# Attention inside a two-layer cross-attention and expert kernel: the transposed-score heads and the P.V groups run four slots behind the plain-score heads of the next batch

## The reference

```python
q = layernorm(x) @ Wq.T ; k = ctx @ Wk.T ; v = ctx @ Wv.T + bv      # 16 heads of 16
scores = einsum('bhsd,bhtd->bhst', qh, kh) / 4                      # masked with -inf
out = einsum('bhst,bhtd->bhsd', softmax(scores), vh)
x = x + tanh(g) * (out @ Wo.T + bo)
```

## Time and profile before

| | us |
|---|---|
| median of three runs (2249.01 to 2251.82) | 2249.69 |
| the profiled execution, own time | 2242.63 |
| its span | 2240.9 |
| layer 0, from the first step's `max_t` to the last one's | 75.2 to 542.6 |
| layer 1, the same | 1057.7 to 1545.8 |
| TensorE busy | 1637.9 (73%) |
| VectorE busy | 1236.0 (55%) |
| ScalarE busy | 665.6 (30%) |
| mean granted TensorE clock | 0.874 of full speed |

### The profile page before, as it was taken

The page is one execution under the profiler, slowest core; times in us unless marked ns, Lnnn a source line. Parts: engine busy times, 40 slices in busy tenths (PEclk is TensorE's granted clock), DMA queues, the critical chain, the costliest instruction groups (busy, mean ns, idle before and its releaser), DMA issues. The chain is left out here.

```text
span 2240.9 us, 44334 instructions
## 1 busy us (share of the span) xinstructions
PE 1637.9 (73%) x14427; PEld 1343.8 (60%) x14428; DVE 1236.0 (55%) x3261; ACT 665.6 (30%) x1299; POOL 724.0 (32%) x620
## 2 busy tenths in 40 slices
PE   3787778887575477735877877787463888896897
PEld 3676667665464355533555555554342888886897
DVE  3565556554466133344656656654465566667664
ACT  2233333333464011111433333343232222221221
POOL 4121112210476455541111111110386533334332
PEclk9989998998898799976888988988676999998999
DMA  3323333321222366644323323320622233332322
GB/s 105 106 88 89 90 104 88 87 78 31 102 94 99 83 116 107 107 91 111 92 84 91 96 78 87 89 74 16 217 78 76 61 66 75 75 75 66 75 35 40
DMA packets 166676, 191.78 MB, mean 86 GB/s; under 512 B 15442, under 2 KB 146868, under 8 KB 166324
## 3 DMA queue, kind: packets, MB, share of 16 engines
q1 hardware_dynamic: 135092, 149.69, 22.9%
q0 software_dynamic: 28416, 40.03, 9.9%
q10 hardware_dynamic: 3072, 0.79, 0.2%
HBM read 113.73 MB, written 75.67 MB: 85 GB/s over the span
## 5 line engine op out<-in xcount | busy, mean ns | idle before, releaser
L629 ACT ACTIVATE a_probs<-a_scores_t 128x384 f32<-128x384 f32 (+1 forms) x512 | 269.7, 545 | 524.7 <-PE a_scores_t L764 262.4
L1714 ACT ACTIVATE e_hidden<-e_h,t_up_bias 128x256 f32<-128x256 f32 x348 | 145.9, 470 | 564.7 <-PE e_h L1748 552.5
L550 DVE TENSOR_REDUCE a_row_max<-a_scores 128x2 f32<-128x512 f32 x256 | 170.3, 679 | 170.5 <-PE a_scores L749 169.0
L407 POOL TENSOR_TENSOR a_rest<-a_qk,a_parts 128x1024 f32<-128x1024 f32 x32 | 68.0, 2125 | 461.6 <-ACT a_parts L582 461.6
L1639 POOL DMA_INDIRECT out_rows<-e_y,e_token x68 | 112.5, 1654 | 309.9 <-DVE e_y L1697 289.9
L1763 PE MATMUL e_y_bank<-e_down_hi,e_hidden_hi 128*128 128x256 f32 x544 | 165.1, 304 | 64.2 <-DVE e_hidden_lo L1670 63.2
L767 PE MATMUL a_scores_t<-a_q_stack,a_k_stack 101*128 101x256 bf16 x512 | 115.7, 315 | 69.0 <-DMA a_q_stack<-a_max_t 67.2
L547 DVE TENSOR_REDUCE a_row_max<-a_scores 128x1 f32<-128x128 f32 x256 | 71.5, 279 | 168.7 <-PE a_scores L746 167.4
L1763 PE MATMUL e_y_bank<-e_down_hi,e_hidden_lo 128*128 128x256 f32 x544 | 159.6, 293 | 0.0
L1763 PE MATMUL e_y_bank<-e_down_lo,e_hidden_hi 128*128 128x256 f32 x544 | 159.4, 293 | 0.0
L1748 PE MATMUL e_h<-e_xs_hi,e_up_hi 128*128 128x256 f32 x544 | 155.9, 287 | 3.1 <-DVE e_xs_lo L1660 1.9
(11 more groups left out here) (257 smaller groups left out, 4539.9 us busy)
## 6 DMA issues: line engine op xcount, KB each, us to landing
parts_dram<-a_parts SPq DMA_DIRECT2D x32, 768.0 KB, 4.1
e_xs_rows<-routed_rows_dram SPq DMA_DIRECT2D x76, 258.0 KB, 2.7
a_q_stack<-parts_dram SPq DMA_DIRECT2D x64, 192.0 KB
a_k_stack<-parts_dram SPq DMA_DIRECT2D x64, 192.0 KB
a_ctx_rows<-in_ctx SPq DMA_DIRECT2D x32, 256.0 KB, 9.1
a_q_stack<-parts_dram SPq DMA_DIRECT2D x64, 128.0 KB
a_k_stack<-parts_dram SPq DMA_DIRECT2D x64, 128.0 KB
t_up<-in_L_ffn_W SPq DMA_DIRECT2D x8, 1024.0 KB, 5.2
```

The source lines that it names most:

```text
L550: nc.vector.reduce_max(row_max[:, :, h], bank[:].rearrange("p (c t) -> p c t", c=TC), AX_X).then_inc(maxed, 1)
L629: nc.scalar.activation(probs[h % NP][:, 0:width], scores_t[h % 2][:, 0:width], ACT.Exp).then_inc(probs_ready, 1)
L1714: nc.scalar.activation(hidden[:, fc, :], h_bank[g][:, at:at + TS], act_func, bias=routed.up_bias[:, bass.ds(e * FC + fc, 1)]).then_inc(hid ...
```

## The change

The transposed heads and everything that hangs on them move four slots back on TensorE; there are now 20 slots, where slots 0 to 3 hold plain heads alone and slots 16 to 19 transposed heads alone. The P.V groups 0, 1 and 2 come in slots 9, 13 and 17. The other parts keep their slot number, so that they stand four transposed heads earlier. ScalarE's parts, which count exponentials, get other numbers to fit, and `cut_hi` comes ahead of all exponentials. VectorE inverts and divides group pair 0 of batch i behind the split of the maxima. POOL waits for its own last result before it writes `rest` again.

```diff
+    LAG = 4
@@ POOL
                     pool.wait_ge(part_hi, b + 1)
+                    need(pool, parts_ready, b)
@@ VectorE
-                if i.has(0):
-                    between |= {14: lambda: invert_dens(0, 0, 0), 15: lambda: (invert_dens(0, 0, 1), divide(0, 0))}
...
+                if i.has(0):
+                    for part in range(TC):
+                        invert_dens(0, 0, part)
+                    divide(0, 0)
@@ ScalarE
-                    between |= {1: lambda: cut_hi(i), 5: lambda: cut_mid(i)}
+                    cut_hi(i)
+                    between |= {1: lambda: cut_mid(i)}
                 if i.has(3):
-                    between |= {8: lambda: evac_xn(i), 10: lambda: evac_ctx(i)}
+                    between |= {4: lambda: evac_xn(i), 6: lambda: evac_ctx(i)}
@@ TensorE
-                for h in range(H):
-                    if i.has(1):
-                        score_head(i, h)
-                    if i.has(0):
+                for slot in range(H + LAG):
+                    if i.has(1) and slot < H:
+                        score_head(i, slot)
+                    h = slot - LAG
+                    if i.has(0) and h >= 0:
                         score_head_t(i, h)
                         if h % GH == 1 and h > GH:
                             mix_group(i, h // GH - 1)
-                    if h in between:
-                        between[h](i)
+                    if slot in between:
+                        between[slot](i)
```

## The result

The changed kernel takes 2243.98 us (median of 20 runs, 2233.37 to 2250.37) where the kernel before took 2249.52 beside it (20 runs): ratio 0.9978, 95% interval 0.9968 to 0.9987. It is 5.5 us faster. The forecast was 17.1 us: the sign was right, the size three times too large. Its profiled execution has a span of 2241.7 us, 0.8 us more than the one of before, so the gain has to be looked for in the attention layers and not in the span.

A forecast was written before the change was run, and what follows sets the result against it. Bound: TensorE's work, its gap awaiting maxima transfers, and low-clock work behind it. Steps of -0.76 us (layer 0) and -0.38 (layer 1), times 15, gave -17.1: 2242.6 to 2225.5 profiled, plus 7.1 is 2232.6; range 2208 to 2252.

The forecast's parts named there:

- what costs nothing: VectorE's moved inversions, `cut_hi` in the gap, POOL's added wait and the changed stack loads on SP: priced at zero.
- What bounds the kernel: In attention steps: TensorE's own work, the gap waiting for maxima transfers, and work slowed by low clock behind it.
- The gap still ends when the transfers land; their issue hangs on `front`, whose place is unchanged.: End of TensorE's gap, before transposed head 0: held fixed, so no cost in the sum.
- The next step's first plain head would wait: Sign of being wrong, at a step's start: plain head 0 waits because half 0 of its stack comes late.
- by up to 0.3 us: Gap end, where transfers land sooner: VectorE's chain ends last instead, by up to this much.
- Four plain heads into the gap: TensorE's gap before transposed head 0: saves 1.16 us a step in layer 0 and 0.88 in layer 1.
- `project_v` loses its cover: TensorE slot 6: new wait for `update_x`, 0.3 us a step in layer 0, 0.4 in layer 1; bounds 0 and 0.9.
- The tail: End of a step: bare transposed heads and group 3 wait for exponentials, 0.3 us (layer 0) and 0.6 (layer 1).
- The clock: Low clock behind the gap: still falls in most steps, some later or shorter; saves 0.2 us a step.
- the band of 0.02 around 0.88: Sign in the profile: mean clock of layer 1 stays at 0.88 within 0.02.
- The clock stays up: Rival: plain heads in the gap keep the clock up; 2166 us in full, chance 0.17 of at least a tenth.
- No change that can be measured: Rival: new waits at `project_v` and in the step's end take the gain back; 2250 us, chance 0.17.
- `project_v`'s wait keeps the clock down: Rival: slot 6 pause lengthens low clock, 1.5 us a step; 2246 us in 20 steps, 2261 in 30; chance 0.11.

The follow-up runs named there:

- e9: Kernel before, with only VectorE's two inversions and the division of batch 0 moved behind the split of the maxima; ratio to before 0.9978.
- e13: Kernel before, with only ScalarE's first cut moved to the head of its step, in the gap, and its second behind exponential 1; ratio to before 1.003.
- e14: Kernel before, with the early first cut and half 0 of the stacks held on SyncE until transposed head 11 is done; ratio to before 0.9991.
- e10: Changed kernel with a lag of two instead of four, v projection in slot 7, evacuations behind exponentials 6 and 8; ratio to before 0.994.
- e16: Kernel before, with steady-step loads of x and ctx issued behind the wait for the parts store, out of the gap; ratio to before 0.9963.
- e17: Kernel before, with x and ctx loads moved out of the gap and eleven unused 512-column matmuls in it; ratio to before 0.9846.
- e11: Changed kernel with the v projection in slot 7 and x and ctx loads behind the wait for the parts store; ratio to before 0.9872.
- e12: Changed kernel with v projection in slot 7, x and ctx loads moved, and eleven unused 512-column matmuls in slots 1 to 4; ratio to before 0.9686.
- e3: Kernel before, with 56 unused 128-column matmuls between plain head 0 and transposed head 0; ratio to before 0.9961.
- e4: Changed kernel with 46 unused 128-column matmuls behind plain heads 1 to 4; ratio to before 0.9862.
- e1: Changed kernel with the v projection one slot later, in slot 7, and its evacuation in slot 8; ratio to before 0.9905.

## Why the prediction was right in sign and wrong in size

*The sign.* In part luck. In the 24 full steps the gain behind the gap and the later end of the gap cancel (-6.1 and +7.0 us). The time was won in the six steps at the ends of the layers, in part by VectorE's inversions behind the split of the maxima. The prediction had put these under "what costs nothing" and looked at a full step, where VectorE idles 3.06 us; in the last two steps of a layer they had held up the split, 5.0 us of waits in all. Alone they give the ratio of the whole change, 0.9978 (e9). How much of the 5.5 us is theirs is not shown, since beside the cut the ratio had nothing of it.

*What bounds the kernel.* Right. The gap and the stretch behind it were the places, and the span could not show the change.

*"The gap still ends when the transfers land; their issue hangs on `front`, whose place is unchanged."* This step failed, and it is where most of the missing gain went: 10.6 us in 30 steps. The issue did stay in place, the landing did not. It has three parts. In layer 0 the last of the three transfers landed 0.29 us later, 4.3 us over 15 steps, since `cut_hi` in the gap, which I had costed at nothing, let the stack loads go sooner (e13, e14). I had followed `cut_hi` on ScalarE alone, and asked of the stacks only whether half 0 could come too late. In the last of the 15 steps of layer 0 plain head 0 waits 4.3 us for its stack and the gap ends at 8.90 us, where it was 6.32: 2.6 us. Before, a wait of 3.5 us for the same stack had no price, for transposed head 0 followed behind one plain head and still waited for the maxima. "The next step's first plain head would wait" for its stack was my sign of being wrong; it came in this step. The rest is VectorE's chain, which ends the gap where the landing is early; I had named that, "by up to 0.3 us", and left it out of the sum. It makes the 0.18 us of layer 1, where the last transfer landed no later than before (6.53 us behind the copy against 6.57).

*Four plain heads into the gap.* Right in kind. The fifth stands before transposed head 0 with a wait of 0.8 us left in the step above, and e10 shows that heads in the gap are worth their price: two fewer, with the tail term halved, cost 8 us.

*`project_v` loses its cover.* Right mechanism, too small: 6.6 us in 12 steps and 9.7 in 13, so 0.44 us over the 15 steps of layer 0 and 0.69 over the 14 in the stretch of layer 1, where 0.3 and 0.4 stood. The difference, 0.14 and 0.29, is 6 us in all. I had set it between 0 and 0.9 by a clock that would often be low at slot 5; in the changed kernel it is low for less time.

*The tail.* 0.3 and 0.6 us a step, 13.5 us in all, forecast; 13 us by ratios, 8 by the steps. Right within what these tell. The waits are seen directly: 0.67 and 1.0 us for the last group, where 0.58 and 0.74 stood.

*The clock.* The low time behind the gap fell by 0.90 and 2.36 us a step, far more than the 0.4 that a term of 0.2 us stands for, and layer 1 left the band of 0.02 around 0.88 that I had given. It did not bring what half its length would be (24 us): with that, the other terms as measured would leave a step behind the gap about 1.0 us shorter (-1.16 + 0.44 + 0.19 - 0.45 and -0.88 + 0.69 + 0.37 - 1.18), and it was 0.51. The fill experiments price low time. In the kernel with moved loads 3.9 us less of it took 1.0 us off the step in either layer (e16 to e17), 0.25 us for each; with the lag 3.3 and 3.8 us less took 1.6 and 1.7 off (e11 to e12), 0.48 and 0.45. Without the lag a faster TensorE only waits longer for VectorE. Its waits for row maxima in layer 0, e16 and then e17:

```profile
PE a_scores L750 <- DVE a_row_max L556: 7.5, 12, 0.7
```

```profile
PE a_scores L750 <- DVE a_row_max L556: 15.7, 26, 0.7
```

So low clock cost the kernel before 0.25 x 4.49 = 1.1 and 0.25 x 6.28 = 1.6 us a step, and costs the changed one about 0.45 x 3.59 = 1.6 and 0.45 x 3.92 = 1.8. Less low time, each microsecond dearer: nothing was won by it. This is worked out from kernels with moved loads and is an estimate for these two. It would explain why e3 and e4, at full clock, show the same picture in their full steps as the kernels themselves.

*The rivals.* "The clock stays up" did not come, except in two steps of layer 0; e12 shows what it would have been. "No change that can be measured" had the new wait of `project_v` about as much too long (0.6 and 0.9 us) as the forecast had it too short, and the tail too long, and it missed the end of the gap as well. The measured ratio, 0.9978, lies just past the 0.2% that I called the limit, near the boundary of two cases. "`project_v`'s wait keeps the clock down" is refuted: e1 removed that wait and the low time stayed (3.45 and 4.26 us against 3.59 and 3.92). Its sum was wrong as well: with 1.5 us lost in 20 steps or in all 30 the forecast of 2232.6 becomes 2263 or 2278, not 2246 or 2261, where the forecast's gain has been taken off twice.

## What to carry to other kernels

A wait that ends with a transfer is not fixed because its issue is: ask of every step that is moved which other loads it lets go sooner, and whether they share the queues with the small transfer on the path; better, move bulk loads out of that window. When work is taken out of a stretch, check each wait in it whose cover that work was, and put its consumer a slot later in the same change (here that alone was worth 16 us, three times what the whole change gained). When a gap is filled, its wait is renamed, not removed: measure from a fixed event to the first instruction behind the gap, and the rest of the step apart. Price the first and the last turns of a software pipeline by themselves: parts are missing in them, so other waits stand open. Of several transfers that one wait needs, read the landing of the last, not the median of all.

## What the runs showed of the hardware that I had not expected

Of three transfers of 8 KB issued one behind the other, the last takes much the longest: in layer 0 of the kernel before it landed 4.9 us after its issue, the first two 2.8 and 2.7, as the profile assigns the landings. With the two 256 KB loads out of the way the median of all three fell from 3.1 to 2.4 us, the last only to 4.7. With the stack loads early and the two loads under way the median was 3.6 to 3.8 us and the last took 5.2 to 5.3.

Eleven matmuls of 512 columns in a gap of about 5 us held the granted clock up in practically all steps of the changed kernel with moved loads and were worth 1.9% (e11 to e12). In the kernel before with moved loads (e17) the same eleven held it up in layer 0, while layer 1 kept 1.97 us low a step. The Trainium skill, "TensorE: Matmul & The Clock Gate", section "Why this matters for your kernels", advises against idle gaps between bursts; e12 agrees where the gap is filled. The changed kernel is where it does not: pauses of mostly 0.8 to 1.0 us, at most 1.4, between single plain heads were followed by low clock in 28 of 30 steps, 3.6 to 3.9 us on average.

Some 50 more instructions in the body of the loop brought TensorE stalls of 3.5 to 5 us, "issue" in the profile, in three steps of layer 0; eleven did not. That the loop's length is the cause was not tested by itself.
